# Products of constants at the beginnings of four stages, and attention's values cleared as GpSimd's first work

## What is computed

```
x  = u
xn = layernorm(x)
x  = x + mamba2(xn) + moe_top1(xn)        # layer 0
xn = layernorm(x)
x  = x + latent_attention(xn) + moe_top2(xn)  # layer 1
```

## Time and profile before

| | |
|---|---|
| median of 3 runs | 2097.98 us (2097.97 to 2099.04) |
| the profiled execution | 2115.85 us |
| its span, first to last instruction | 2114.1 us |
| mean granted TensorE clock | 0.931 of full speed |
| PE busy | 1805.7 us, 85% of the span, 9950 matmuls |
| DVE busy | 1376.7 us, 65% |
| ACT busy | 1158.1 us, 55% |
| POOL busy | 419.7 us, 20% |
| state-space stage | about 93.8 to 760 us |
| first expert stage | about 760 to 1067 us |
| projection | about 1173.6 to 1276 us |
| attention and second experts | about 1276.6 us to the end |

### The profile page before, as it was taken

One profiled execution on the slowest core, in us unless ns is written; L12 is line 12 of the kernel. 1 busy time (PEld: TensorE's weight loads), 2 busy tenths in 40 slices (PEclk: granted clock), 3 DMA queues, 4 the chain that ended last, 5 costly groups with the idle time before them and its releaser, 6 DMA issues. The chain is left out here.

```text
span 2114.1 us, 33649 instructions
## 1 busy us (share of the span) xinstructions
PE 1805.7 (85%) x9950; PEld 1230.2 (58%) x9950; DVE 1376.7 (65%) x3090; ACT 1158.1 (55%) x2806; POOL 419.7 (20%) x406
## 2 busy tenths in 40 slices
PE   5288898898899869899945695998989999999998
PEld 2246666656656669799932353564646565655555
DVE  5647667667667622122246686797878888888885
ACT  2154654664564612122212354888788888788886
POOL 2003313313413432422111202010010202020101
PEclk9589999999999989899977797999999999999999
DMA  4411211211211168455354294233333334333311
GB/s 168 147 59 62 89 63 66 94 65 59 100 68 50 60 223 281 161 175 175 131 160 160 75 296 130 70 82 72 98 72 85 98 84 104 80 91 81 81 31 31
DMA packets 143789, 226.10 MB, mean 107 GB/s; under 512 B 17725, under 2 KB 110015, under 8 KB 143648
## 3 DMA queue, kind: packets, MB, share of 16 engines
q1 hardware_dynamic: 124464, 179.95, 27.4%
q0 software_dynamic: 19184, 44.45, 8.2%
HBM read 174.26 MB, written 50.99 MB: 107 GB/s over the span
## 5 line engine op out<-in xcount | busy, mean ns | idle before, releaser
L2271 DVE TENSOR_SCALAR att_scores<-att_psS 128x512 f32<-128x512 f32 x512 | 349.6, 683 | 106.3 <-PE att_psS L2103 90.9
L2220 ACT ACTIVATE att_prob<-att_scores,att_shift 128x512 f32<-128x512 f32 x512 | 383.2, 748 | 30.7 <-DVE att_shift L2287 30.6
L2229 ACT COPY att_pT<-att_psT 128x512 f32<-128x512 f32 x512 | 305.9, 598 | 136.1 <-PE att_psT L2111 134.9
L2279 DVE CUSTOM_DVE_ANT_0 att_scores<-att_scores,first_decay 128x512 f32<-128x512 f32 x512 | 348.4, 681 | 0.0
L2111 PEld LDWEIGHTS att_psT<-ident,att_prob 128*128 128x128 f32 x2048 | 244.8, 142 | 159.4 <-issue 100.2
L2111 PE MATMUL att_psT<-ident,att_prob 128*128 128x128 f32 x2048 | 315.2, 277 | 15.4 <-ACT att_pT L2229 13.9
L2103 PE MATMUL att_psS<-first_ks,first_qs 128*128 128x512 bf16 x512 | 197.7, 387 | 27.8 <-DVE att_scores L2271 22.6
L1113 ACT ACTIVATE mamba_L<-mamba_am,mamba_minus 128x128 f32<-128x128 f32 x512 | 153.9, 388 | 59.3 <-PE mamba_psY L986 59.2
L2125 PE MATMUL att_psO<-att_pT,att_v 128*32 128x512 f32 x1024 | 139.7, 619 | 37.7 <-ACT att_pT L2229 37.7
L1488 PE MATMUL ffn_psH<-ffn_xT,ffn_w 128*128 128x128 f32 x1248 | 151.0, 280 | 5.0 <-issue 4.4
L1488 PEld LDWEIGHTS ffn_psH<-ffn_xT,ffn_w 128*128 128x128 f32 x1248 | 150.1, 196 | 8.6 <-issue 6.7
(11 more groups left out here) (283 smaller groups left out, 2820.8 us busy)
## 6 DMA issues: line engine op xcount, KB each, us to landing
ffn_w<-in_w SPq DMA_DIRECT2D x39, 1024.0 KB
mamba_am<-a_rows SPq DMA_DIRECT2D x64, 512.0 KB, 3.8
first_qs<-q_parts SPq DMA_DIRECT2D x256, 64.0 KB
first_ks<-k_parts SPq DMA_DIRECT2D x256, 64.0 KB
xn<-xn_all SPq DMA_DIRECT2D x16, 512.0 KB, 5.8
ffn_w<-in_w POOLq DMA_DIRECT2D x8, 1024.0 KB, 6.1
att_w<-in_inter POOLq DMA_DIRECT2D x7, 1024.0 KB, 5.6
att_w<-in_outer POOLq DMA_DIRECT2D x7, 1024.0 KB
```

The lines of the kernel that those rows point to most:

```text
L2220: nc.scalar.activation(prob[:, n % NP], scores[:, n % NCL], ACT.Exp, bias=shift[:, h % 2, t:t + 1], accum_out=total[:, octet % 2, t, j, i: ...
L2229: nc.scalar.copy(pT[:, h % HEADS_T, :, t * P:(t + 1) * P], bank_of("turn", n)[:].rearrange("p (k q) -> p k q", k=CPB)).then_inc(pT_ready, 1)
L2271: vec.tensor_scalar(scores[:, n % NCL], psS[n % NS][:], -CLAMP, CLAMP, ALU.max, ALU.min).then_inc(clipped, 1)
L2279: vec.tensor_tensor_reduce(scores[:, n % NCL], scores[:, n % NCL], decay[:, FAR - t * P:FAR - t * P + SEQ], 1.0, -2.0 * CLAMP, ALU.mult, A ...
```

## The change

A helper `keep_running` issues products of `C.ones` and `C.ident`, into a PSUM bank that the stage later begins with `start=True`, and nobody reads them. It is called at the beginning of TensorE's list in `mamba` (16 products), in `one_expert_each` (16) and in `project` (14), and in `attend_and_experts` behind the third score (14). In attention GpSimd's clear of `v` is moved ahead of its loads, and VectorE's wait for it is moved from before its first step to the first spreading of values.

```diff
--- before.py
+++ after.py
@@ -101,6 +101,13 @@
 
 class Constants:
     pass
+
+
+def keep_running(nc, C, bank, times):
+
+
+    for _ in range(times):
+        nc.tensor.matmul(bank, C.ones[:], C.ident[:], start=True, stop=True)
 
 
 class Choice:
@@ -880,6 +887,7 @@
 
             @block.tensor
             def _(pe):
+                keep_running(nc, C, psO[0][:, 0:P], 16)
                 for q in range(2):
                     table.multiply(nc, pe, psP, 0, q)
                 pe.wait_ge(conv_in, 3 * 16)
@@ -1503,6 +1511,7 @@
                                               start=(f == 0), stop=(f == FT - 1))
                     mm.then_inc(down_done, 1)
 
+                keep_running(nc, C, psY[0][:, 0:P], 16)
                 turn_x(0)
                 for j in range(N + 1):
                     if j < N:
@@ -1722,6 +1731,7 @@
                             mm = nc.tensor.matmul(psV[g][:, t], latT[:, b % 2, (2 * g + t) * P:(2 * g + t + 1) * P], wuv[:], start=True, stop=True)
                         mm.then_inc(v_done, 1)
 
+                keep_running(nc, C, psV[0][:, 0, 0:P], 14)
                 pe.wait_ge(joined, 1)
                 pe.wait_ge(kvd_in, 3 * 16)
                 for k in range(KD):
@@ -2066,10 +2076,10 @@
                                    accum_op=ALU.add).then_inc(sums_added, 16)
                     added[1] += 1
 
+                nc.gpsimd.memset(v[:], 0.0).then_inc(v_cleared, 1)
                 load_rows(0)
                 load_w1(0)
                 load_w2(0)
-                nc.gpsimd.memset(v[:], 0.0).then_inc(v_cleared, 1)
                 for n in range(-SCORE, LAST):
                     e = last_job_at(n, "turn", 2)
                     if e is not None and e + 1 < L1_EXPERTS:
@@ -2194,6 +2204,8 @@
                         turn(n)
                     if 0 <= n + SCORE < N:
                         score(n + SCORE)
+                        if n + SCORE == NS - 1:
+                            keep_running(nc, C, psF[:, 0:P], 14)
                     for k in range(CPB):
                         if group_at(n, MIX + k) is not None:
                             mix(group_at(n, MIX + k), k)
@@ -2289,6 +2301,8 @@
                 def spread_values(b):
 
                     dve.wait_ge(first.v_in, (b + 1) * 16)
+                    if b == 0:
+                        dve.wait_ge(v_cleared, 1)
                     if b >= 2:
 
                         dve.wait_ge(mixed, (b - 1) * GROUPS)
@@ -2339,7 +2353,6 @@
                         vec.tensor_scalar(y[:, t], psF[:, 0:D], places.weight[:, e * RT + t:e * RT + t + 1], None, ALU.mult).then_inc(y_ready, 1)
 
                 dve.wait_ge(first.decay_ready, 1)
-                dve.wait_ge(v_cleared, 1)
                 for n in range(-SCORE, LAST):
                     if 0 <= n + CLIP < N:
                         clip(n + CLIP)
```

## The result

| | before | changed |
|---|---|---|
| median of 4 runs each | 2098.23 us | 2079.61 us (2076.34 to 2081.26) |
| ratio | | 0.9909, 95% interval 0.9891 to 0.9926 |
| profiled execution | 2115.85 us | 2078.79 us |
| mean granted clock | 0.931 | 0.947 |
| repeat 1 | 2096.41 us | 2085.79 us, ratio 0.9949 (0.9933 to 0.9965) |

What follows compares the result with a forecast made beforehand. Bound: the chain of waits ending in attention, so gains at stage beginnings count in full. Terms -6.4 - 2.7 + 2 - 1.5 = -8.6 us, from 2097.98 to 2089.4 us; range 2083 to 2095.

Steps and rivals of the forecast that it cites:

- Attention's beginning: Attention, first score to fourth clip: clear moved and products added bring the clip to +7.3, gain 6.4 us (5.4 to 8.4).
- Projection: Projection's beginning: real products start 1.0 us late but run at the higher clock, net gain 2.7 us.
- Expert stage: First experts: faster up step only lengthens the idle wait for GpSimd's mark, 2 us lost (nothing to 3.2).
- The stall of the earlier trace: Expert stage, 849.26 to 872.47: TensorE waiting for its own issue, 15.9 us taken as absent from the median.
- the slower rival: TensorE's issue: 60 more products bring the stall into the timed executions, price 15.9 us, 2105.3 us; chance 0.05.
- State-space stage: Its beginning: clock holds through the pause and 1.5 us of the table, gain 1.5 us (0 to 5.5), carried.
- "Carried", in attention: Attention's gain of 6.4 us reaches the end in full; rival that it is not carried: 2095.8 us, chance 0.10.
- The rival of the held clock: State-space stage: products keep 2.4 GHz through table and convolutions, gain 5.5 there, 2085.4 us in all; chance 0.15.

Runs made afterwards that it cites:

- before_again: The kernel before, unchanged, measured again: 2093.07 us, ratio 0.9988.
- both_wide: `fill_pause` with the table's 39 columns taken three times and the factors' 8 columns twelve times: 2085.75 us, ratio 0.9865.
- mamba_only: The kernel before with only the 16 products of the state-space stage: 2104.91 us, ratio 0.9959.
- products_only: The changed kernel with GpSimd's clear and VectorE's wait left where they were before, all four groups of products kept: 2104.95 us, ratio 0.9965.
- table_wide: `fill_pause` with the table's 39 columns in the state-space stage taken three times: 2096.56 us, ratio 0.9927.
- fill_pause: The changed kernel without products in expert stage and attention, with 24 instead of 16 in the state-space stage: 2074.52 us, ratio 0.9898.

## Why the prediction was right and wrong

- **Attention's beginning: right.** Clear alone 10.9 (10.5 said), fourth clip at 6.97, 6.61 and 6.65 (7.3), products 4.2 (4), rows turned at 20.26 us (20.5). The 28 records took 5.48 us (5.4). From the fourth clip to VectorE's first write of `att_oT` 63.67 us passed in the profile of before and 63.68 after: carried one for one up to there. Over all profiles it is 63.7 in eleven and 65.3 to 65.4 in three, `before_again` and `both_wide` among them, so this difference isn't the change's.
- **Projection: right.** First take 12.24 us after the stage's start (12.5 to 13 said; 15.42 before). The stage gained 2.7 us in the first profile, 1.2 to 2.7 over the five above (2.7 said). Over all profiles it took 100.1 to 101.1 us in the nine with products there and 101.8 to 103.5 in the five without, 2.5 apart in the mean.
- **Expert stage: right in mechanism and size.** Idle time 3.40 (3.5), down step slower than 3.72, price 0 to 3.1 (2, bounds 0 and 3.2). The row of the table grew by more (372.5 to 373.1 against 369.13). From the stage's start to the start of normalise it took 306.1 us in `before_again` and 307.6, 309.2 and 307.5 in the changed kernel, which is the price of the first tile and nothing else. The rest lies in normalise, 63.0 against 65.1, 63.9 and 65.0; that stage took 61.6 to 65.1 over all profiles, with and without products (64.1 in the first profile of before).
- **The stall of the earlier trace rows: right.** It took 17.6 us in the profile (15.9 said), it was in no median of this comparison, and the slower rival, that the new products bring it on, fell: kernels with and without products had it in two sets and neither in the two others.
- **State-space stage: the step that failed.** Its term was 1.5 us; the first profile has 7.1 to 8.3 us less than the two of before (658.2 against 665.3 and 666.5), so 5.6 to 6.8 of the 10.0 us by which the first result missed the forecast lie here. "I take it that the clock holds through the pause and the first 1.5 us of the table and is then lost: gain 1.5 us ... VectorE's taps follow one another from 113.24 on, so it is carried." The first half is one case of three, and it left out that the clock could be back during the convolutions. The first taps came at 15.47, 18.75 or 17.09 us in three profiles of one kernel, against 19.38 and 18.81: 3.3 to 3.9, 0.1 to 0.6 or 1.7 to 2.3 us earlier. Where a fall lands against the stage's start differs from execution to execution, and a single profile of before shows one of these places. The second half missed that the rest of the stage is no constant either. It took 642.69, 646.91 and 642.72. `mamba_only` alone gave 8.1 us by its median (5.9 to 11.4) where 1.5 stood in the sum. Over all profiles the taps came at 15.47 in three of the seven with 16 products, at 18.75 in three and at 17.09 in one, and at 18.6 to 19.4 in the four without: 1.8 us earlier in the mean. The case that the prediction took is the one with 17.09: there the clock held through the pause and 1.3 us of the table and was then at 0.50 for 6.8 us. That 1.5 lies near the mean of the three cases is luck, and the term as a whole was too small by what the rest of the stage gave.
- **"Carried", in attention.** From the fourth clip to the end five profiles with the old beginning took 820.7 to 825.8 us and nine with the clear moved 817.8 to 824.6. The means, 823.5 and 820.2, are 3.3 apart, but the ranges overlap, and the length goes with the clock rather than with the clear: nine profiles with 24.8 to 32.6 us at 0.50 in this part took 817.8 to 820.9, and five with 37.3 to 47.6 took 822.3 to 825.8. `products_only`, with the clear late, is among the nine (32.2 us, 820.7), and `both_wide`, with it early, among the five (43.0, 824.6). That the change brings the shorter ones is not shown. The sum had nothing for this.

With the means of the profiles (before's two against the changed kernel's three, the expert stage against `before_again` alone) the sum reads: ahead -0.5, state-space -4.7, experts and normalise +3.6, routing +0.1, projection -2.0, attention -9.8 (-6.9 to the fourth clip, -2.9 behind it), together -13.3 instead of -8.6; the three medians mean -14.7. So the beginnings were sized well, and the sum was short by the state-space term (3.2) and by attention's rest (2.9). The range failed with it: its lower end was made from the beginnings' bounds only, though the earlier trace rows already showed the clock falling in the steady part of the state-space stage. For the first result a part stays open even so: its profile is 14.2 us shorter than that of `before_again`, and its medians are 18.6 apart.

The rival of the held clock is partly right. The clock held for most of the table in the changed kernel's first profile, but in no profile into the convolutions until the table's products were widened. The Trainium skill, "TensorE: Matmul & The Clock Gate", section "What's actually happening", has activity release the throttle; the runs agree for the wide products (3.82 of 3.82 us busy with 117 columns, the clock at 1.00 and still there behind them) and disagree for the narrow ones, where a TensorE busy 3.41 of 3.41 us was followed by 0.50.

**Left open.** Whether the 16 products make the shorter rest of the state-space stage (642) likelier: it came in 3 of 7 profiles of kernels with them, in none of 3 without them and not in the one with 24 products (the kernels with widened products left out). In those three the factors of the first two sequences lie 76.7 to 76.9 us apart, in the others 78.4 to 79.2. Open as well are why the median of `mamba_only` gained twice what its profile shows, and what the 8 further products of `fill_pause` gained. More profiles of each would be needed, and these were not taken.

## What to carry to other kernels

Read the granted clock behind each narrow stretch of TensorE, not only behind its pauses: here widening 8 moving columns to 96 with copies of themselves cost 0.07 us a sequence and gave 10.9 us, where the whole change gave 10.6 to 18.6. Before filling a pause ahead of a step, look at what ends the next wait; if it is another engine (GpSimd's mark in the expert stage), the gain can turn into idle time and a lower clock. Where the clock falls in a steady loop, one profile gives a stage's time only to some microseconds, and the range of a forecast has to hold that.

## What was not expected of the hardware

- The same kernel's stage took 658.16, 665.66 and 659.81 us in three executions, and the clock fell at other places in each: 61.4 us at 0.50 behind the first taps in two of them and 64.8 in the other, and a table of 4.12, 6.81 or 5.86 us.
- A stall of TensorE's own issue, 16 to 19 us in the first expert stage, came in all profiles of two sets and in none of the two others, one of them on the same chip.
- A gain at a beginning can be undone downstream: `table_wide` was 1.45 us earlier at its first taps and 6.8 us longer at the lower clock after them.
